# M's tiles as two 64-row products on the halves of the array, ahead of a burst of layer 0

## What is computed

```python
x = x + L0(x, itok_B_0_7)          # x: 128 batches of 64 x 512
x = x + L1(x, itok_B_0_6)
# L0: w = weights[subject]         8 subjects of 64 x 64
#     einsum('bct,bcd->bdt', x, w) + bias[subject][:, :, None]
# L1: einsum('btd,od->bto', x, W)  W is 512 x 512
#     + (x A[adapter]^T) Bm[adapter]^T * scalings[adapter]
#       8 adapters, A 16 x 512, Bm 512 x 16
```

## Time and profile before

| | |
|---|---|
| time, median of 3 runs | 254.08 us (253.62 to 254.99) |
| profiled execution | 255.75 us, its span 254.0 us |
| PE busy | 238.5 us, 94% of the span |
| DVE, ACT, POOL busy | 138.9, 111.4, 79.6 us |
| moved by DMA | 36.68 MB |
| granted clock of PE | 0.996 of full speed |

### The profile page before, as it was taken

How to read it: one execution, slowest core, us unless ns; L and a number is a source line. 1 busy time by engine, 2 the same in 40 slices (tenths; PEclk the granted TensorE clock), 3 DMA queues, 4 the chain that set the end, 5 groups by cost and what they waited for, 6 DMA issues and landing times.

```text
span 254.0 us, 9847 instructions
## 1 busy us (share of the span) xinstructions
PE 238.5 (94%) x2932; PEld 196.1 (77%) x2933; DVE 138.9 (55%) x241; ACT 111.4 (44%) x189; POOL 79.6 (31%) x283
## 2 busy tenths in 40 slices
PE   1888998999999999999999999999999999999993
PEld 1767885888878887888878887878878888888882
DVE  5277567666475656565574757474774745243300
ACT  2262544443643536353634435353535434342511
POOL 4367520355006510454015700466342413000000
PEclk9999999999999999999999999999999999999998
DMA  6745364464646564555646463655547364641331
GB/s 174 177 148 166 107 185 101 120 181 127 206 102 196 131 180 134 141 156 152 191 103 199 131 194 95 171 143 162 165 124 207 101 198 119 201 123 54 85 83 41
DMA packets 24147, 36.68 MB, mean 144 GB/s; under 512 B 6594, under 2 KB 6594, under 8 KB 24130
## 3 DMA queue, kind: packets, MB, share of 16 engines
q1 hardware_dynamic: 17536, 27.28, 39.2%
q10 hardware_dynamic: 6594, 9.18, 12.6%
HBM read 19.66 MB, written 16.78 MB: 143 GB/s over the span
## 4 chain that ended last, share of the span: by engine, by line
PE 85%; issue 3%; DVE 2%; POOL 1%; POOLq 1%; ACT 1%; ACTq 1%; DVEq 0%
PE ps L782 70%; PE ps L761 13%; PE ps L737 2%; PE ps L701 1%; POOLq L227 1%; POOL bias_pair L377 1%; POOL p_pair L366 1%; DVE m_f L486 1%; ACT x_hi L598 1%; DVE m_lo L492 0%; ACTq L624 0%; DVE x_lo L518 0%; DVE a_parts L473 0%; ACT m_hi L592 0%; DVE b_parts L479 0%
## 5 line engine op out<-in xcount | busy, mean ns | idle before, releaser
L782 PE MATMUL ps<-m_hi,x_hi 128*128 x264 | 105.8, 401 | 0.0
L782 PE MATMUL ps<-m_hi,x_lo 128*128 x264 | 103.3, 391 | 0.0
L782 PE MATMUL ps<-m_lo,x_hi 128*128 x264 | 103.3, 391 | 0.0
L518 DVE TENSOR_TENSOR x_lo<-x,x_hi 128x512 fp32r<-128x512 f32 x64 | 44.7, 698 | 80.4 <-ACT x_hi L598 80.3
L366 POOL COPY p_pair<-p_all 64x64 f32 x128 | 42.3, 331 | 126.0 <-issue 77.3
L598 ACT ACTIVATE x_hi<-x 128x512 fp32r<-128x512 f32 x64 | 40.4, 632 | 46.7 <-DVE x L510 28.2
L607 ACT ACTIVATE o_ring<-ps 128x512 f32<-128x512 f32 x60 | 35.7, 596 | 57.1 <-PE ps L782 56.9
L782 PEld LDWEIGHTS ps<-m_hi,x_hi 128*128 128x128 f32 x264 | 49.8, 189 | 11.1 <-issue 0.2
L782 PEld LDWEIGHTS ps<-m_hi,x_lo 128*128 128x128 f32 x264 | 49.8, 189 | 10.7
L782 PEld LDWEIGHTS ps<-m_lo,x_hi 128*128 128x128 f32 x264 | 49.9, 189 | 9.8
L510 DVE TENSOR_TENSOR x<-ps,bias_pair 128x512 f32<-128x512 f32 x64 | 43.6, 682 | 5.6 <-PE ps L761 5.6
(11 more groups left out here) (90 smaller groups left out, 62.3 us busy)
## 6 DMA issues: line engine op xcount, KB each, us to landing
x_ring<-in_x_dram SPq DMA_DIRECT2D x128, 128.0 KB, 2.7
out_dram<-o_ring SPq DMA_DIRECT2D x64, 128.0 KB, 2.3
out_dram<-o_ring ACTq DMA_DIRECT2D x64, 128.0 KB, 2.4
a_f<-in_L_cond_A_dram SPq DMA_DIRECT2D x8, 128.0 KB
o_ring<-in_L_cond_W_dram SPq DMA_DIRECT2D x2, 256.0 KB, 4.6
o_ring<-in_L_cond_W_dram ACTq DMA_DIRECT2D x2, 256.0 KB, 5.6
b_nat<-in_L_cond_Bm_dram ACTq DMA_DIRECT2D x1, 256.0 KB, 3.5
p_all<-in_L_cond_weights_dram SPq DMA_DIRECT2D x2, 128.0 KB, 6.7
```

The lines of the kernel that those rows point to most:

```text
L518: nc.vector.tensor_tensor(x1_lo[:, u % HELD], x1[:, u % 2], x1_hi[:, u % HELD], ALU.subtract).then_inc(x1_lo_ready, 1)
L782: mm = nc.tensor.matmul(ps[:, bank, :], part[:, u % HELD, c, :], m[:, ds(k * (TC * T) + c * T, T)], start=(c == 0 and part is x1_hi and m ...
```

## The change

The 128 rows now hold eight copies of A's and Bm's rows instead of four and zeros. Both halves hold the same four layouts. Each product reads 64 rows: even chunks the lower half, odd chunks the upper. The products come in twos, both ahead of a burst: at u = 5 chunks 0 and 1, at u = 1 chunks 2 and 3. The `m_add`s and `m_round`s move with them, and the `m_split`s go to u = 6 (chunks 0, 1) and u = 4 (chunks 2, 3). In the head, chunks 0 and 1 come at j = 1 and chunks 2 and 3 at j = 3. POOL writes twice as much in `dup_b` and loses the memsets and selects that made `neg` and the zeros; DVE makes `neg` with four small operations. The load of `a_f` goes from 64 rows to 128.

```diff
-    G = 4
-    GR = G * R
+    G = 8
+    ROWS = 4 * R
...
-        a_f = sb("a_f", [GR, T])
+        a_f = sb("a_f", [P, T])
...
-                return {5: [(n + 2, 0)], 7: [(n + 2, 1)], 1: [(n + 2, 2)], 3: [(n + 2, 3)]}.get(u, [])
-            return {1: [(1, 0)], 2: [(1, 1), (1, 2)], 3: [(1, 3)]}.get(j, [])
+                return {5: [(n + 2, 0), (n + 2, 1)], 1: [(n + 2, 2), (n + 2, 3)]}.get(u, [])
+            return {1: [(1, 0), (1, 1)], 3: [(1, 2), (1, 3)]}.get(j, [])
...
-                return {4: [(n + 1, 3)], 6: [(n + 2, 0)], 0: [(n + 2, 1)], 2: [(n + 2, 2)]}.get(u, [])
-            return {2: [(1, 0)], 3: [(1, 1), (1, 2)]}.get(j, [])
+                return {4: [(n + 1, 2), (n + 1, 3)], 6: [(n + 2, 0), (n + 2, 1)]}.get(u, [])
+            return {2: [(1, 0), (1, 1)]}.get(j, [])
...
-            nc.gpsimd.memset(neg[:], 0.0).then_inc(consts, 1)
...
-            nc.gpsimd.memset(b_dup[:], 0.0).then_inc(consts, 1)
-            pool.wait_ge(consts, 12)
-            nc.gpsimd.memset(a_parts[GR:P, :].bitcast(F32), 0.0).then_inc(consts, 1)
...
-                nc.gpsimd.tensor_tensor(b_dup[:, :, 0:G, :],
+                nc.gpsimd.tensor_tensor(b_dup[:],
...
+            did(nc.vector.tensor_scalar(low_i[:, 0:1], pid_i[:], 2 * R, None, ALU.bitwise_and))
+            low_done = did(nc.vector.tensor_scalar(low_i[:, 1:2], pid_i[:], R, None, ALU.bitwise_and))
...
+            did(nc.vector.tensor_scalar(neg[:, 0:1], low_i[:, 0:1], -1.0 / (2 * R), None, ALU.mult))
+            neg_done = did(nc.vector.tensor_scalar(neg[:, 1:2], low_i[:, 1:2], -1.0 / R, None, ALU.mult))
...
-                nc.vector.scalar_tensor_tensor(out=a_parts[0:GR, :], in0=a_parts[0:GR, :], scalar=neg[0:GR, 0:1], in1=a_f[:],
+                nc.vector.scalar_tensor_tensor(out=a_parts[:], in0=a_parts[:], scalar=neg[:, 0:1], in1=a_f[:],
...
+                    m_split(K * TC - 2, TC - 2)
                     m_split(K * TC - 1, TC - 1)
...
-                nc.tensor.matmul(ps[:, 4 + chunk % 2, :], a_parts[:, chunk * P:chunk * P + P], b_parts[:],
+                rows = slice(ROWS * (chunk % 2), ROWS * (chunk % 2) + ROWS)
+                nc.tensor.matmul(ps[:, 4 + chunk % 2, :], a_parts[rows, chunk * P:chunk * P + P], b_parts[rows, :],
                                  start=True, stop=True).then_inc(m_summed, 1)
...
             m_product_first(2)
+            m_product_first(3)
             first_inputs(0)
             layer0(0, 0)
-            m_product_first(3)
```

More of the change, by code:

```diff
@@ L39, in cond_residual_layers @@
     TC = T // P
-    G = 4
-    GR = G * R
-    assert 2 * C == P and T % P == 0 and T * 4 == 2048 and GR <= 64 and K == S == 8
+    G = 8
+    ROWS = 4 * R
+    assert 2 * C == P and T % P == 0 and T * 4 == 2048 and G * R == P and ROWS == C and K == S == 8
     PAIRS = B // 2
@@ L71, in cond_residual_layers @@
         b_parts = sb("b_parts", [P, T], F32R)
-        a_f = sb("a_f", [GR, T])
+        a_f = sb("a_f", [P, T])
         a_parts = sb("a_parts", [P, T], F32R)
         b_nat = sb("b_nat", [P, K, TC * R])
-        b_dup = sb("b_dup", [P, TC, P // R, R])
+        b_dup = sb("b_dup", [P, TC, G, R])
         x_ring = sb("x_ring", [P, XR, T])
@@ L97, in cond_residual_layers @@
         neg = sb("neg", [P, 2])
+        low_i = sb("low_i", [P, 2], I32)
         iota_i = sb("iota_i", [P, B], I32)
@@ L308, in _ @@
                                     pattern=[[-1, P]], channel_multiplier=1).then_inc(consts, 1)
-            nc.gpsimd.memset(neg[:], 0.0).then_inc(consts, 1)
[L311 to L322, removed]
-            nc.gpsimd.memset(b_dup[:], 0.0).then_inc(consts, 1)
-            pool.wait_ge(consts, 12)
-            nc.gpsimd.memset(a_parts[GR:P, :].bitcast(F32), 0.0).then_inc(consts, 1)
-            pool.wait_ge(consts, 13)
             pool.wait_ge(bnat_in, 16)
@@ L412, in _ @@
             nc.vector.tensor_tensor(ident_halves[:], ident[:, 0:C], ident[:, C:2 * C], ALU.add).then_inc(consts_b, 1)
+            need(low_done)
+            did(nc.vector.tensor_scalar(neg[:, 0:1], low_i[:, 0:1], -1.0 / (2 * R), None, ALU.mult))
+            neg_done = did(nc.vector.tensor_scalar(neg[:, 1:2], low_i[:, 1:2], -1.0 / R, None, ALU.mult))
             dve.wait_ge(ids_in, 16)
@@ L519, in x1_split @@
                                         ALU.subtract).then_inc(x1_lo_ready, 1)
-            dve.wait_ge(consts, 13)
+            need(neg_done)
             b_split(0)
@@ L573, in a_round @@
                 at_least(act, m_summed, i * TC)
-                nc.scalar.activation(a_parts[0:GR, :], a_f[:], ACT.Copy).then_inc(a_rounded, 1)
+                nc.scalar.activation(a_parts[:], a_f[:], ACT.Copy).then_inc(a_rounded, 1)
             def b_round(i):
@@ L730, in m_product_first @@
                     pe.wait_ge(wt_copied_too, chunk - 1)
-                nc.tensor.matmul(ps[:, FIRST + chunk, :], a_parts[:, chunk * P:chunk * P + P], b_parts[:],
+                rows = slice(ROWS * (chunk % 2), ROWS * (chunk % 2) + ROWS)
+                nc.tensor.matmul(ps[:, FIRST + chunk, :], a_parts[rows, chunk * P:chunk * P + P], b_parts[rows, :],
                                  start=False, stop=True, skip_group_check=True).then_inc(m_summed, 1)
```

## The result

The changed kernel takes 257.03 us (median of 5 runs, 254.93 to 257.53), the kernel before beside it 254.40. The ratio is 1.0084, 95% interval 1.0052 to 1.0115: slower, by about 2 us. The prediction said 254.5, 253.3 to 256.1, and "within 0.5%" as the likeliest. It was wrong.

What follows compares the result with a forecast made beforehand. PE was taken to bound B6 to B2, ACT then DVE B2 to B6, and POOL the start. The terms +0.5 - 0.38 - 0.66 + 1.2 - 0.23 = +0.43 on 254.08 gave 254.5, range 253.3 to 256.1.

Steps and rivals of the forecast that it cites:

- B2 to B6, +0.24 each: Half-body set by ACT, then DVE: an added m_split costs 0.61, a removed m_round saves 0.37; five halves, +1.2.
- The rival of a fixed issue cost: The 0.38 ahead of B6 is fixed issue, not DVE's; those halves save 0.11 each, giving 252.8; chance 0.10.
- The head, -0.38: From the head's B2 to the first B6: ACT's last round 0.99 earlier, an extra m_split takes 0.61 back.
- B6 to B2, -0.11 each: Half-body set by PE: overlapping 64-row products save 0.23, tiling adds 0.12; six halves, -0.66.
- 0.12 of added cost: In each half from B6 to B2: 0.09 for a tiling change plus 0.03 for the second product's start.
- the rival of serial products: The two 64-row products run one behind the other: 0.23 more per half to B2, +1.4, 255.9; chance 0.14.
- The tail, -0.23: From the last B2 to the tail's burst, set by PE: the half loses its product, 0.23.
- The start, "+0.5": Ahead of layer 1: dup_b(1) grows by 0.66 in POOL's chain, partly returned by PE's rate; bounds 0.33 and 0.66.
- The third rival: Start later than POOL's 0.66: a_f lands over 1.8 us later, or PE's rate rises later; 255.7; chance 0.12.

Runs made afterwards that it cites:

- split_later: The changed kernel with the splits of chunks 2 and 3 moved from u = 4 to u = 5, behind the add B6 waits for: 251.74, 0.9879.
- b_dup8: The kernel before with dup_b writing all eight groups at places 0 and 1: 255.65, 1.0051.
- b_load8: The kernel before with a_f loaded as eight copies, 256 KB, of which the lower 64 rows are used: 254.51, 0.9999.
- The two sets of runs: The changed kernel measured twice against the kernel before: 257.03, 1.0084 in the first set; 256.15, 1.0042 in the second.
- dup_later: The changed kernel with its later splits (split_later) and dup_b(1) moved behind pair 3's copies: 251.44, 0.9860; the same kernel again 250.66, 0.9844.

## Why the prediction was wrong

- **B2 to B6, +0.24 each: right.** 14.77 from burst to burst against a forecast of 14.8, five halves +1.15 against +1.2, the add's end plus 0.71 in every body, and `split_later` removed the wait. The rival of a fixed issue cost is out. PE's side of it was too short: it was to be ready 0.11 earlier and came 0.11 later, as the two products ahead of B6 start 0.12 to 0.19 apart (0.003 ahead of B2) and the last one lasts 0.49. So the "issue" rose to 0.51 rather than 0.7, which costs nothing.
- **The head, -0.38: right.** 15.95 against 16.33, and the first `m_add` of place 1's second two chunks came 8.2 behind the head's B2, where 8.1 was worked out; `turn_b(2)` waited 0.73 for the `m_add`, hidden as said.
- **B6 to B2, -0.11 each: this step failed in its size.** Measured -0.01 to -0.08, together -0.29 instead of -0.66. "0.12 of added cost" should have been 0.20. The overlap was right (0.233 a pair), the rival of serial products is out. The prediction priced one more change of tiling at 0.09, by the change of another pair of tilings, and 0.03 for the second product's start. The change was 0.09, and the second product's start next to nothing. What the sum left out is the first product behind a change: its weight load is no longer hidden, and it holds PE 0.10 longer. The rule of the Trainium skill, "TensorEngine Tiling (Array Packing)", Key Properties, that a change of mode drains TensorE, was weighed at +0.4 us over six halves. The trace agrees in kind: 0.09 at each change of mode and 0.003 between the two halves.
- **The tail, -0.23:** -0.29 (13.13 instead of 13.42 from the last B2 to the next burst).
- **The start, "+0.5": this step failed, and made most of the miss.** The doubled `dup_b(1)` costs 1.04 - 0.61 = 0.43 of queue, less than the 0.66 taken from L348, but `b_dup8` costs about 1.2 in all. I had let PE's lower rate hand half of the delay back; in the profiles it took 0.7 more, which is likely and not shown. The third rival named the rate's later rise, at 0.12, with 1.2 us over the forecast; it came to 0.6 to 0.7 over. Of its two mechanisms the load of `a_f` is out (`b_load8`).

By the measured terms: +1.1 for the start, -0.38, -0.29, +1.15, -0.29, +1.3 in all, where the prediction had +0.43. The two sets of runs, together +1.6, bear that out within their intervals. On the 254.08 that the prediction started from, +1.3 is 255.4, still inside its range. The 257.03 lies outside because more came on top: the kernel before stood at 254.40 beside it, and the first set was the high one of the two, +2.1 by its ratio, with three of five executions at the low mean clock. Whether that share is the start's doing or chance is open. The range took in the bounds of the tiling and 0.5 to 0.9 for the runs' spread, but not a set as high as this.

## What to carry to other kernels

A wait that looks like "issue" ahead of a burst is worth following to the last semaphore in front of it: here one line moved behind the add gave about 3 us without the change around it and 4 us with it. Count every change of the array's tiling, and with each one the first matmul behind it, whose weights come late: in and out of 64 x 128 between full matmuls cost 0.46 us, twice a 128 x 512 product, and next to 64 x 64 tiles still 0.20, so halving two products saved 0.02. In a start where PE's rate has not settled, a delay on another engine may cost more than its length (0.43 of queue, about 1.2 us in the runs); one profile cannot tell, and here seventeen only made it likely.

## What the runs showed that I had not expected

- Four 64-row products queued on one half and then four on the other took 1.14 us ahead of B2, the same as in turns (1.13), with matmuls of the upper half starting ahead of lower ones that stand before them in the program.
- The first 12 matmuls of layer 1, the same work at the same place in the program, took 3.0 to 5.4 us from one profile to the next; for one and the same kernel, `dup_later` and `dup_later_again`, 5.03 and 3.00.
- The granted clock is shown as 1.00 throughout the start of the kernel before, while its matmuls there ran at half rate (records of 0.63 against 0.39). The first record of the clock in that trace lies at 23.1 us; ahead of it the 1.00 stands for a missing record. The mean clock of an execution therefore did not tell how long PE was slow.
- A wide `dup_b` of 512 elements took 1.04, and L348 of 512 elements, another operation of the same kind on the same engine, 1.27.
